# Attention block on one core: the mask instruction scales and keeps the negated maximum itself, its semaphore counts tiles, and the output banks are drained in two parts

## The chip, the core and the metric

The kernel runs on one core of a Trainium2 chip. The metric is the device time of one execution in microseconds, taken as the median of repeated runs. The engines named below are PE (TensorE, matrix products), DVE (VectorE), ACT (ScalarE), POOL (GpSimd) and SP (SyncE, which issues the DMAs). Each works through its own instructions in order, and they meet only at semaphores.

## What is computed

The reference is one transformer layer with modulation: layer norm, attention with 32 query heads that share 8 key and value heads, an output projection, a second layer norm, and a mixture of 64 expert biases chosen by the top 8 of a router. x is 4 x 512 x 512 in float32. This is the part that matters here (names shortened):

```python
q = (h @ Wq.T)            # 4 x 512 x (32 x 128), then rotary
k = rope part of (h @ Wkr.T) and (h @ Wdk.T) @ Wupk.T
v = (h @ Wdk.T) @ Wupv.T
scores = einsum('bhqd,bhkd->bhqk', q, k) / sqrt(128)
scores = where(causal, scores, -1e9)
attn = softmax(scores)
out = einsum('bhqk,bhkd->bhqd', attn, v) @ Wo.T
x = x + ga * out
# then layer norm, router softmax, top 8, x + gb * ffn
```

## The kernel before

Every float32 product is made of three products of a high and a low part (hi and lo tiles; `passes`), so each 128x512 product of PE comes three times. The work is laid out by hand as one long pipeline: 128 steps, one for each pair of batch (4) and query head (32). Step `t` belongs to unit `u = t // 4` (one key and value head of one batch) and has `h = t % 4` (the query head within the unit). The rows `MEMSET wait_slot` (L1082) are tiny instructions that carry the wait for PE's scores.

In step `t` the engines do, in this order:

- PE: the scores of tile t+1, in four pieces by query block 3, 2, 1, 0 with 512, 384, 256 and 128 keys (L460; PSUM banks s3, s2, and s1 for the last two); the query projection of tile t+3 into bank s3 (`q_proj`, L407, 12 matmuls); in steps with h = 0 a transpose of v and the key projection of the next unit (L439, L418), with h = 2 its value projection (L430); the output projection of tile t-2 into banks o0 to o3 (`out_head`, L516, summed over the unit's four heads); and the values of tile t-1 (L501, bank pv).
- DVE: `mask_and_max(t+1, 0)` (query blocks 3 and 2), the low part of the attention output of tile t-2 (OT_lo, L1118), `mask_and_max(t+1, 1)` (blocks 1 and 0), the reciprocal of the row sums (L1093), the rotary products of tile t+3 (`q_rope`, L1055 to L1057), with h = 0 also v_lo and the key's rotary products, then the 32x32 transposes of the probabilities (L1110, L1112), and with h = 1 `add_out(u-1)`: four adds that drain banks o0 to o3 into `y` (L1126).
- ACT: OT_hi (L824), PT_hi, the high part of the transposed probabilities (L820), the four exponentials of tile t+1 (L797), their normalisation (L804), qT_hi (L774), and in ten steps of each group of 16 the high part of a block of the next weights (L768).
- POOL: PT_lo in two pieces (L1451), the sum of the rotary products (L1440), qT_lo (L1445), key work, and the low part of a block of the next weights (wq_lo and others, L1436).
- SP: the transposed probabilities make a round trip through DRAM (stored at L1642, read back into PT_raw in four DMAs at L1651, after POOL has finished with PT_raw).

`mask_and_max` is where the change lies. For each query block one custom DVE instruction (L1083) reads the score bank, adds the mask, writes `probs` and keeps the row maximum, which a small read-accumulator instruction then writes to `row_max`. After two blocks the semaphore `dve_s` rises by one (two per tile), DVE waits for it itself, and a `TENSOR_SCALAR` (L1087) on two columns makes `neg_max`, which ACT waits for by `dve_nm`. PE waits for `dve_s` before it writes a bank again: for `q_proj(t+3)`, which needs s3 alone, the wait is `dve_s >= 2 * (t + 1) + 1`, and so for blocks 3 and 2 together.

From step 117 on (`FFN_FROM`) the router and expert work of one 128-row tile is woven into each step. The last three tiles are transposed by PE instead of DVE and DMA (`last_step`), and a tail of router work ends the program.

Of the kernel before, what the change touches and what calls it, by code (L numbers as in the profile page):

```python
# [12 lines left out]
P = 128  # L13
# [86 lines left out]
def build(nc, A, out):  # L100
    ctx = ExitStack()
    with ctx:
# [4 lines left out]
        class Region:  # L107
# [51 lines left out]
        rot_s = whole.take("rot_s", [P, SEQ])  # L159
        row_max, neg_max, row_sum, row_inv = (  # L160
            [whole.take(f"{n}{i}", [P, QT]) for i in range(2)] for n in ("row_max", "neg_max", "row_sum", "row_inv"))
        router_bias = whole.take("router_bias", [P, EXPERTS])
# [125 lines left out]
        def sem(name):  # L288
# [27 lines left out]
                                                  sem("act_o"))  # L316
        dve_s, dve_nm, dve_ri, dve_r, dve_o = (sem("dve_s"), sem("dve_nm"), sem("dve_ri"),
                                                      sem("dve_r"), sem("dve_o"))
# [19 lines left out]

        FFN_FROM = ALL - STEPS + GROUP + 1

        def pieces(t):
# [11 lines left out]
        def tensor_program(pe):  # L353
# [43 lines left out]
            def q_proj(t):  # L397
                b, h = t // GROUP % BATCH, t % GROUP
                if t > 0:
                    pe.wait_ge(dve_r, t)  # L400
                if t >= 3:
                    pe.wait_ge(dve_s, 2 * (t - 2) + 1)
                if b == 0:
                    pe.wait_ge(pool_w, chunk_event(t // STEPS - 1, CHUNKS.index(f"wq{h}")) + 1)
                for c in range(CH):
                    for n, (w, x) in enumerate(passes(wq, hT)):
                        mm = pe.matmul(q_bank(t)[:], w[:, h, c, :], x[:, b * CH + c, :],  # L407
                                       start=(c == 0 and n == 0), stop=(c == CH - 1 and n == 2))
                mm.then_inc(pe_qp, 1)

            def k_proj(u):
                if u > 0:
                    pe.wait_ge(dve_s, 2 * (GROUP * (u - 1) + 1) + 1)
                if u % BATCH == 0:
                    pe.wait_ge(pool_w, chunk_event(u // BATCH - 1, CHUNKS.index("wk")) + 1)
                for c in range(CH):
                    for n, (w, x) in enumerate(passes(wk, hT)):
                        mm = pe.matmul(kv_bank(u)[:], w[:, c, :], x[:, (u % BATCH) * CH + c, :],  # L418
                                       start=(c == 0 and n == 0), stop=(c == CH - 1 and n == 2))
                mm.then_inc(pe_k, 1)  # L420

            def v_proj(u):
                pe.wait_ge(dve_kr, u + 1)
                if u > 0:
                    pe.wait_ge(dve_s, 2 * (GROUP * (u - 1) + 3) + 1)
                if u % BATCH == 0:
# [7 lines left out]
            def v_transpose(u):  # L434
                pe.wait_ge(act_vraw, u + 1)
                if u > 0:
                    pe.wait_ge(dve_s, 2 * (GROUP * u + 1) + 2)
                for j in range(QT):
                    mm = pe.transpose(vt_bank(u)[:, j * P:(j + 1) * P], kv_raw[:, j * P:(j + 1) * P], ident[:])  # L439
                mm.then_inc(pe_vt, 1)  # L440

            def scores(t, tiles):
                if tiles[0] == QUERY_ORDER[0]:
# [3 lines left out]
                    if t > 0:  # L447
                        pe.wait_ge(dve_s, 2 * t)
                    if t >= 2:
# [117 lines left out]
            def step(t):  # L567
# [15 lines left out]
                if n is not None:  # L583
                    pe.wait_ge(dve_s, 2 * (t + 2))
                    if h == 0:
# [17 lines left out]
            def last_step(t):  # L603
# [20 lines left out]
                values(t)  # L624
                pe.wait_ge(dve_s, 2 * (t + 2 if has1 else t + 1))
                ffn_mix(n - 4, "s3")
# [93 lines left out]
        def scalar_program(act):  # L720
# [72 lines left out]
            def exponentials(t, half):  # L793
                m = t % 2
                act.wait_ge(dve_nm, 2 * t + half + 1)
                for qt in HALVES[half]:
                    ins = act.activation(row(t, qt), row(t, qt), ACT.Exp, bias=neg_max[m][:, qt:qt + 1], scale=SCALE,  # L797
                                         accum_out=row_sum[m][:, qt:qt + 1])
                ins.then_inc(act_exp, 1)
# [179 lines left out]
        def vector_program(dve):  # L979
# [93 lines left out]
            def mask_and_max(t, half):  # L1073
# [5 lines left out]
                for qt in HALVES[half]:  # L1079
                    if qt:  # L1080
                        dve.wait_ge(pe_s, 4 * t + (4 if qt == 1 else 4 - qt))
                        dve.memset(wait_slot[:, qt:qt + 1], 0.0)  # L1082
                    ins = dve.tensor_tensor_reduce(row(t, qt), score_bank[qt], mask[:, SEQ - (qt + 1) * P:], 1.0, LOWEST,  # L1083
                                                   ALU.add, ALU.max, row_max[m][:, qt:qt + 1])
                ins.then_inc(dve_s, 1)
                dve.wait_ge(dve_s, 2 * t + half + 1)
                dve.tensor_scalar(neg_max[m][:, half_cols(half)], row_max[m][:, half_cols(half)], -SCALE, None,  # L1087
                                  ALU.mult).then_inc(dve_nm, 1)

# [30 lines left out]

            def add_out(u):
                for j in range(QT):
                    ps = out_bank(u, j)
# [129 lines left out]
            def step(t):  # L1253
# [5 lines left out]
                if n is not None:  # L1259
                    ffn_norm(n - 1)  # L1260
                invert_sums(t + 1, 0)
                q_rope(t + 3)
# [12 lines left out]
                if h == 1 and u > 0 and not soon(t - 1):  # L1275
                    add_out(u - 1)
                if soon(t):
# [518 lines left out]
```

## Time and profile before

| | us |
|---|---|
| median of 3 runs | 1674.41 (1671.79 to 1675.16) |
| the profiled execution | 1675.79 |
| its span, first to last instruction | 1674.5 |
| PE busy (share of the span) | 1548.9 (92%) |
| DVE busy | 1272.3 (76%) |
| POOL busy | 1027.2 (61%) |
| ACT busy | 1002.1 (60%) |

A profile gives for each engine the time in which it worked, for groups of equal instructions the count, the busy time and the idle time of the engine just before them, and for a stretch of time each instruction with its start and length. Lengths of matmuls overlap, since the engine is pipelined: the distance between two starts tells what one costs.

### The profile page before, as it was taken

Reading aid. Unit: us, or ns where it says so; the run is one execution under the profiler, and the core shown is the slowest. Engines: PE = TensorE matmul, PEld = TensorE weight load, DVE = VectorE, ACT = ScalarE, POOL = GpSimd, SP = SyncE. Lnnn points to the kernel's source line nnn. Section 1 sums busy time; section 2 is a strip of 40 time slices with the busy share of each in tenths; the row PEclk is TensorE's granted clock in tenths of the full one; section 3 lists DMA queues with packets and bytes.
Section 4 is the critical chain, followed back from the end, with each engine's and each line's share of the span. In section 5 each row is a group of like instructions: output and inputs, shape, how many; then the busy total and the mean of one; then the engine's idle time right before and its main releaser. Section 6 shows DMA issues by size and latency. Waiting matters only on the chain.

```text
span 1674.5 us, 24760 instructions
## 1 busy us (share of the span) xinstructions
PE 1548.9 (92%) x7630; PEld 1294.0 (77%) x7630; DVE 1272.3 (76%) x3663; ACT 1002.1 (60%) x2333; POOL 1027.2 (61%) x774
## 2 busy tenths in 40 slices
PE   8989999999999999999999999999999999897787
PEld 5668888888888888888888888888888888676664
DVE  6867777777777777777777787777777777678698
ACT  3356667666666566666666666666665666554341
POOL 2756566655665566656666566556665566577664
PEclk9989999999999999999999999999999999999877
DMA  8434344443444344433444344434443344534311
GB/s 309 165 117 130 111 136 137 130 133 107 140 151 124 110 131 130 149 111 118 150 129 123 126 128 137 137 110 131 136 133 129 113 134 151 153 104 136 98 50 71
DMA packets 139123, 218.30 MB, mean 130 GB/s; under 512 B 29472, under 2 KB 101920, under 8 KB 138992
## 3 DMA queue, kind: packets, MB, share of 16 engines
q1 hardware_dynamic: 138672, 216.61, 41.1%
q8 instruction: 62, 1.02, 0.3%
q14 instruction: 69, 0.57, 0.1%
q10 hardware_dynamic: 320, 0.11, 0.0%
HBM read 127.38 MB, written 89.29 MB: 129 GB/s over the span
## 4 chain that ended last, share of the span: by engine, by line
PE 65%; DVE 21%; issue 10%; POOL 2%; ACT 1%; DMA 1%; DVEq 0%; SPq 0%; POOLq 0%; ACTq 0%
PE bank_s L407 22%; PE bank_o L516 14%; PE bank_pv L501 10%; PE bank_s L418 5%; PE bank_s L430 5%; PE bank_s L460 5%; DVE y L1126 4%; DVE probs L1083 3%; DVE blocks L1110 3%; DVE rot_s L1056 2%; DVE rot_c L1055 2%; DVE rot_s L1057 1%; PE bank_s L393 1%; DVE row_max L1083 1%; PE bank_s L439 1%
## 5 line engine op out<-in xcount | busy, mean ns | idle before, releaser
L1451 POOL TENSOR_TENSOR PT_lo<-PT_raw,PT_hi 128x640 fp32r<-128x640 f32 x250 | 386.2, 1567 | 122.9 <-ACT PT_hi L820 122.9
L797 ACT ACTIVATE probs<-probs,neg_max 128x512 f32<-128x512 f32 x508 | 281.3, 555 | 183.3 <-DVE neg_max L1087 173.8
L1440 POOL TENSOR_TENSOR rot_c<-rot_c,rot_s 128x512 f32<-128x512 f32 x128 | 167.1, 1305 | 275.1 <-DVE rot_s L1057 275.1
L804 ACT ACTIVATE probs<-probs,row_inv 128x512 f32<-128x512 f32 x508 | 255.2, 553 | 83.1 <-DVE row_inv L1093 83.1
L407 PE MATMUL bank_s<-hT_lo,wq_hi 128*128 128x512 f32 x500 | 207.2, 414 | 70.3 <-DVE row_max L1083 62.8
L1083 DVE CUSTOM_DVE_ANT_0 probs<-bank_s,mask 128x512 f32<-128x512 f32 x508 | 229.1, 486 | 0.1
L1445 POOL TENSOR_TENSOR qT_lo<-rot_c,qT_hi 128x512 fp32r<-128x512 f32 x128 | 166.9, 1304 | 92.8 <-ACT qT_hi L774 92.8
L1110 DVE STREAM_TRANSPOSE blocks<-probs 128x384 f32<-128x384 f32 x500 | 202.8, 443 | 6.0 <-ACT probs L804 2.9
L407 PE MATMUL bank_s<-hT_hi,wq_hi 128*128 128x512 f32 x500 | 196.4, 393 | 0.0
L516 PE MATMUL bank_o<-wo_lo,OT_hi 128*128 128x512 f32 x496 | 193.4, 390 | 3.1 <-DVE OT_lo L1118 3.1
L407 PE MATMUL bank_s<-hT_hi,wq_lo 128*128 128x512 f32 x500 | 196.2, 392 | 0.0
L516 PE MATMUL bank_o<-wo_hi,OT_hi 128*128 128x512 f32 x496 | 193.0, 389 | 0.0
L516 PE MATMUL bank_o<-wo_hi,OT_lo 128*128 128x512 f32 x496 | 193.0, 389 | 0.0
L1082 DVE MEMSET wait_slot<- 128x1 f32 x384 | 22.7, 59 | 217.8 <-PE bank_s L460 217.7
L824 ACT ACTIVATE OT_hi<-bank_pv 128x512 fp32r<-128x512 f32 x124 | 74.3, 599 | 186.3 <-PE bank_pv L501 186.3
L501 PE MATMUL bank_pv<-PT_lo,v_hi 128*128 128x512 f32 (+3 forms) x512 | 168.1, 328 | 15.2 <-POOL PT_lo L1451 6.6
L407 PEld LDWEIGHTS bank_s<-hT_lo,wq_hi 128*128 128x128 f32 x500 | 94.5, 189 | 99.6 <-issue 83.9
L820 ACT ACTIVATE PT_hi<-PT_raw 128x640 fp32r<-128x640 f32 x250 | 169.6, 729 | 0.3 <-DMA PT_raw<-blocks 0.3
L460 PE MATMUL bank_s<-kT_lo,qT_hi 128*128 128x512 f32 (+3 forms) x512 | 160.8, 314 | 8.7 <-issue 3.7
L501 PE MATMUL bank_pv<-PT_hi,v_lo 128*128 128x512 f32 (+3 forms) x512 | 168.1, 328 | 0.0
L501 PE MATMUL bank_pv<-PT_hi,v_hi 128*128 128x512 f32 (+3 forms) x512 | 167.8, 328 | 0.0
L460 PE MATMUL bank_s<-kT_hi,qT_lo 128*128 128x512 f32 (+3 forms) x512 | 166.7, 326 | 0.0
(224 smaller groups left out, 3627.6 us busy)
## 6 DMA issues: line engine op xcount, KB each, us to landing
blocks<-blocks SPq DMA_DIRECT2D x125, 640.0 KB, 2.9
PT_raw<-blocks SPq DMA_DIRECT2D x500, 160.0 KB, 3.1
stage<-in_wq SPq DMA_DIRECT2D x32, 256.0 KB, 3.5
stage<-in_wo SPq DMA_DIRECT2D x32, 256.0 KB, 3.5
wmod<-in_wmod SPq DMA_DIRECT2D x6, 1024.0 KB, 10.1
y<-in_x SPq DMA_DIRECT2D x4, 1024.0 KB, 12.2
stage<-in_x SPq DMA_DIRECT2D x16, 256.0 KB, 2.8
out_y<-h SPq DMA_DIRECT2D x16, 256.0 KB, 2.0
```

Of the source, the lines that this page charges most:

```text
L407: mm = pe.matmul(q_bank(t)[:], w[:, h, c, :], x[:, b * CH + c, :], start=(c == 0 and n == 0), stop=(c == CH - 1 and n == 2))
L460: mm = pe.matmul(score_bank[qt], q[:, qt * P:(qt + 1) * P], k[:, 0:(qt + 1) * P], start=(n == 0), stop=(n == 2))
L501: mm = pe.matmul(to, a[:, kb, :], ps, start=(kb == 0 and n == 0), stop=(kb == KEY_ORDER[-1] and n == 2))
L516: mm = pe.matmul(out_bank(u, j)[:], o[:, j * P:(j + 1) * P], w[:, h, :], start=(h == 0 and n == 0), stop=(h == GROUP - 1 and n == 2))
L797: ins = act.activation(row(t, qt), row(t, qt), ACT.Exp, bias=neg_max[m][:, qt:qt + 1], scale=SCALE, accum_out=row_sum[m][:, qt:qt + 1])
L804: ins = act.activation(row(t, qt), row(t, qt), ACT.Copy, scale=row_inv[t % 2][:, qt:qt + 1])
L820: act.activation(PT[0][:, at], PT_raw[:, at], ACT.Copy).then_inc(act_t, 1)
L1083: ins = dve.tensor_tensor_reduce(row(t, qt), score_bank[qt], mask[:, SEQ - (qt + 1) * P:], 1.0, LOWEST, ALU.add, ALU.max, row_max[m][:, qt ...
L1110: ins = dve.transpose(blocks_v[:, qt:qt + 3 * whole_keys - 2:3], keys[:, 0:whole_keys])
L1440: pool.tensor_tensor(rot_c[:], rot_c[:], rot_s[:], ALU.add).then_inc(pool_a, 1)
L1445: pool.tensor_tensor(lo[:], rot_c[:], hi[:].bitcast(F32), ALU.subtract).then_inc(pool_q, 1)
L1451: pool.tensor_tensor(PT[1][:, at], PT_raw[:, at], PT[0][:, at].bitcast(F32), ALU.subtract).then_inc(pool_t, 1)
```

## The change

The custom instruction scales by minus the softmax scale and keeps a running minimum, so that its accumulator already is the negated, scaled maximum; the two `TENSOR_SCALAR` per tile and the semaphore `dve_nm` are gone, and the exponentials take scale -1. `dve_s` now rises by one after each query block (four per tile); `score_read(t, qt)` is the count at which block `qt` of tile `t` has been read, and all waits are written by it. Each exponential has its own wait. `add_out` drains banks o0 and o1 where it stood (h = 1), and banks o2 and o3 one step later (h = 2), between the masks and the reciprocal.

```diff
+        def score_read(t, qt):
+
+            return QT * (t + 1) - qt
...
             def q_proj(t):
                 if t >= 3:
-                    pe.wait_ge(dve_s, 2 * (t - 2) + 1)
+                    pe.wait_ge(dve_s, score_read(t - 2, 3))
...
             def k_proj(u):
                 if u > 0:
-                    pe.wait_ge(dve_s, 2 * (GROUP * (u - 1) + 1) + 1)
+                    pe.wait_ge(dve_s, score_read(GROUP * (u - 1) + 1, 2))
...
             def v_transpose(u):
                 if u > 0:
-                    pe.wait_ge(dve_s, 2 * (GROUP * u + 1) + 2)
+                    pe.wait_ge(dve_s, score_read(GROUP * u + 1, 0))
...
             def exponentials(t, half):
                 m = t % 2
-                act.wait_ge(dve_nm, 2 * t + half + 1)
                 for qt in HALVES[half]:
-                    ins = act.activation(row(t, qt), row(t, qt), ACT.Exp, bias=neg_max[m][:, qt:qt + 1], scale=SCALE,
+                    act.wait_ge(dve_s, score_read(t, qt))
+                    ins = act.activation(row(t, qt), row(t, qt), ACT.Exp, bias=row_min[m][:, qt:qt + 1], scale=-1.0,
                                          accum_out=row_sum[m][:, qt:qt + 1])
                 ins.then_inc(act_exp, 1)
...
             def mask_and_max(t, half):
...
                         dve.memset(wait_slot[:, qt:qt + 1], 0.0)
-                    ins = dve.tensor_tensor_reduce(row(t, qt), score_bank[qt], mask[:, SEQ - (qt + 1) * P:], 1.0, LOWEST,
-                                                   ALU.add, ALU.max, row_max[m][:, qt:qt + 1])
-                ins.then_inc(dve_s, 1)
-                dve.wait_ge(dve_s, 2 * t + half + 1)
-                dve.tensor_scalar(neg_max[m][:, half_cols(half)], row_max[m][:, half_cols(half)], -SCALE, None,
-                                  ALU.mult).then_inc(dve_nm, 1)
+
+                    dve.tensor_tensor_reduce(row(t, qt), score_bank[qt], mask[:, SEQ - (qt + 1) * P:], -SCALE,
+                                             -LOWEST, ALU.add, ALU.min, row_min[m][:, qt:qt + 1]).then_inc(dve_s, 1)
...
-            def add_out(u):
-                for j in range(QT):
+            def add_out(u, tiles=range(QT)):
+                for j in tiles:
...
             def step(t):
                 mask_and_max(t + 1, 1)
                 if n is not None:
                     ffn_norm(n - 1)
+                if h == 2 and u > 0 and not soon(t - 2):
+                    add_out(u - 1, range(2, QT))
                 invert_sums(t + 1, 0)
...
                 if h == 1 and u > 0 and not soon(t - 1):
-                    add_out(u - 1)
+                    add_out(u - 1, range(2))
```

What this makes of the order of DVE's instructions, first where a step with h = 1 ends and the step with h = 2 begins. "ISA probs,row_max" is the mask instruction and the "ISA row_max" behind it the read of its accumulator. Before:

```order
L1126 TENSOR_TENSOR y<-bank_o,y 128x512 [waits pe_op] x4
L1082 MEMSET wait_slot 128x1 [waits pe_s,dve_tp]
L1083 ISA probs,row_max_93<-bank_s,mask 128x512
L1083 ISA row_max_93 128x1
L1082 MEMSET wait_slot 128x1 [waits pe_s]
L1083 ISA probs,row_max_93<-bank_s,mask 128x384
L1083 ISA row_max_93 128x1
L1087 TENSOR_SCALAR neg_max_95<-row_max_93 128x2 [waits dve_s]
L1118 TENSOR_TENSOR OT_lo<-bank_pv,OT_hi 128x4x4x32 [waits act_o]
L1082 MEMSET wait_slot 128x1 [waits pe_s]
L1083 ISA probs,row_max_93<-bank_s,mask 128x256
L1083 ISA row_max_93 128x1
```

And after:

```order
L1127 TENSOR_TENSOR y<-bank_o,y 128x512 [waits pe_op] x2
L1086 MEMSET wait_slot 128x1 [waits pe_s,dve_tp]
L1088 ISA probs,row_min_93<-bank_s,mask 128x512
L1088 ISA row_min_93 128x1
L1086 MEMSET wait_slot 128x1 [waits pe_s]
L1088 ISA probs,row_min_93<-bank_s,mask 128x384
L1088 ISA row_min_93 128x1
L1119 TENSOR_TENSOR OT_lo<-bank_pv,OT_hi 128x4x4x32 [waits act_o]
L1086 MEMSET wait_slot 128x1 [waits pe_s]
L1088 ISA probs,row_min_93<-bank_s,mask 128x256
L1088 ISA row_min_93 128x1
```

Two of the four adds stand ahead of the masks instead of four, and the `TENSOR_SCALAR` between block 2 and OT_lo is gone.

Further on in the step with h = 2, DVE before (the rows from block 0 to the first rotary product):

```order
L1083 ISA probs,row_max_93<-bank_s,mask 128x128
L1083 ISA row_max_93 128x1
L1087 TENSOR_SCALAR neg_max_95<-row_max_93 128x2 [waits dve_s]
L1093 RECIPROCAL row_inv_99<-row_sum_97 128x2 [waits act_exp]
L1055 TENSOR_TENSOR rot_c<-bank_s,cos_t 128x512 [waits pool_q,pe_qp]
```

And after:

```order
L1088 ISA probs,row_min_93<-bank_s,mask 128x128
L1088 ISA row_min_93 128x1
L1127 TENSOR_TENSOR y<-bank_o,y 128x512 [waits pe_op] x2
L1094 RECIPROCAL row_inv_97<-row_sum_95 128x2 [waits act_exp]
L1059 TENSOR_TENSOR rot_c<-bank_s,cos_t 128x512 [waits pool_q,pe_qp]
```

The two other adds stand between the last mask and the reciprocal, ahead of the rotary products.

ACT, the exponentials of one tile, before:

```order
L820 ACTIVATE PT_hi<-PT_raw 128x640 [waits pe_pv,d_tr0]
L820 ACTIVATE PT_hi<-PT_raw 128x640
L797 ACTIVATE probs,row_sum_96<-probs,neg_max_94 128x512 [waits dve_nm]
L797 ACTIVATE probs,row_sum_96<-probs,neg_max_94 128x384
L797 ACTIVATE probs,row_sum_96<-probs,neg_max_94 128x256 [waits dve_nm]
```

And after:

```order
L824 ACTIVATE PT_hi<-PT_raw 128x640 [waits pe_pv,d_tr0]
L824 ACTIVATE PT_hi<-PT_raw 128x640
L801 ACTIVATE probs,row_sum_94<-probs,row_min_92 128x512 [waits dve_s]
L801 ACTIVATE probs,row_sum_94<-probs,row_min_92 128x384 [waits dve_s]
L801 ACTIVATE probs,row_sum_94<-probs,row_min_92 128x256 [waits dve_s]
```

The exponential of block 2 has a wait of its own (as has that of block 0), and each waits for `dve_s`.

## Rows read from the trace of the kernel before

**Rows 1.** The page: span, chain of work that ended last, PE's longest group with its idle time.

```profile
span 1674.5 us, 24760 instructions
...
PE 65%; DVE 21%; issue 10%; POOL 2%; ACT 1%; DMA 1%; DVEq 0%; SPq 0%; POOLq 0%; ACTq 0%
...
L407 PE MATMUL bank_s<-hT_lo,wq_hi 128*128 128x512 f32 x500 | 207.2, 414 | 70.3 <-DVE row_max L1083 62.8
```

**Rows 2.** Groups by line, 400 to 1400 us: busy, mean ns, idle before and releasers.

```profile
L407 PE MATMUL bank_s<-hT_lo,wq_hi 128*128 128x512 f32 x348 | 143.2, 412 | 47.8 <-DVE row_max L1083 41.4 <-issue 3.7 <-POOL wq_lo L1436 2.7
...
L1087 DVE TENSOR_SCALAR neg_max<-row_max 128x2 f32<-128x2 f32 x174 | 95.3, 548 | 6.0
```

**Rows 3.** Timeline of all engines in a step with h = 1: start, length, instruction.

```profile
710.75 0.69 DVE L1083 CUSTOM_DVE_ANT_0 probs<-bank_s,mask 128x512 f32<-128x512 f32 x1
...
711.37 0.08 DVE L1083 DVE_READ_ACCUMULATOR2_ANT row_max<- 128x1 f32 x1
711.38 0.55 DVE L1083 CUSTOM_DVE_ANT_0 probs<-bank_s,mask 128x384 f32<-128x384 f32 x1
...
711.46 0.27 PE L460 MATMUL bank_s<-kT_hi,qT_hi 128*128 128x128 f32 x1
711.86 0.08 DVE L1083 DVE_READ_ACCUMULATOR2_ANT row_max<- 128x1 f32 x1
...
712.09 0.48 PE L407 MATMUL bank_s<-hT_lo,wq_hi 128*128 128x512 f32 x1 [0.35 <-DVE row_max L1083]
...
712.40 0.40 PE L407 MATMUL bank_s<-hT_hi,wq_lo 128*128 128x512 f32 x1
```

**Rows 4.** Timeline of all engines where the next step, h = 2, begins.

```profile
719.01 2.45 DVE L1126 TENSOR_TENSOR y<-bank_o,y 128x512 f32<-128x512 f32 x4
...
721.32 0.27 PE L460 MATMUL bank_s<-kT_hi,qT_hi 128*128 128x128 f32 x1
721.39 0.69 DVE L1083 CUSTOM_DVE_ANT_0 probs<-bank_s,mask 128x512 f32<-128x512 f32 x1
...
722.00 0.08 DVE L1083 DVE_READ_ACCUMULATOR2_ANT row_max<- 128x1 f32 x1
...
722.72 0.47 PE L407 MATMUL bank_s<-hT_lo,wq_hi 128*128 128x512 f32 x1 [1.12 <-DVE row_max L1083]
```

**Rows 5.** Timeline where step 64 (h = 0) begins, with its weight block.

```profile
835.53 1.28 POOL L1436 TENSOR_TENSOR wq_lo<-stage,wq_hi 128x512 fp32r<-128x512 f32 x1
...
836.23 0.27 PE L460 MATMUL bank_s<-kT_hi,qT_hi 128*128 128x128 f32 x1
...
836.96 0.48 PE L407 MATMUL bank_s<-hT_lo,wq_hi 128*128 128x512 f32 x1 [0.46 <-POOL wq_lo L1436]
```

**Rows 6.** Timeline of all engines around one of the small scaling instructions.

```profile
353.22 3.07 POOL L1451 TENSOR_TENSOR PT_lo<-PT_raw,PT_hi 128x640 fp32r<-128x640 f32 x2 [0.41 <-ACT PT_hi L820]
...
354.75 1.56 DVE L1087 TENSOR_SCALAR neg_max<-row_max 128x2 f32<-128x2 f32 x1
```

**Rows 7.** That instruction by its line, whole run: minimum, median, maximum ns.

```profile
L1087 DVE TENSOR_SCALAR neg_max<-row_max x256: 168/348/1616, 91.3 to 1605.0; 128x2 f32<-128x2 f32 x128
```

**Rows 8.** Another DVE instruction that reads a bank, with two operations, by tile.

```profile
L1036 DVE TENSOR_SCALAR h_raw<-bank_o,modT x8: 777/796/812, 31.3 to 96.4; 128x512 f32<-128x512 f32 x8
```

**Rows 9.** Timeline of DVE: the first rotary product of the step of rows 3.

```profile
715.14 0.69 DVE L1055 TENSOR_TENSOR rot_c<-bank_s,cos_t 128x512 f32<-128x512 f32 x1 [0.69 <-PE bank_s L407]
```

**Rows 10.** The DMAs that read PT_raw back, by line: lengths and time to landing.

```profile
L1651 SPq DMA_DIRECT2D PT_raw<-blocks x500: 302/426/1941, 104.0 to 1566.8; - x167
...
DMA to landing us min/median/max: 2.5/3.1/4.7
```

**Rows 11.** The chain of waits in the router stage at the end.

```profile
1514.21 1.05 DVE neg_max L1087
...
1546.93 1.04 DVE neg_max L1087
```

**Rows 12.** The subtraction of the router's norm on DVE, by line: minimum, median, maximum ns.

```profile
L1165 DVE TENSOR_SCALAR h<-y,small x10: 535/1549/1873, 1469.2 to 1612.8; 128x512 f32<-128x512 f32 x10
```

More of the change, by code:

```diff
@@ L159, in build @@
         rot_s = whole.take("rot_s", [P, SEQ])
-        row_max, neg_max, row_sum, row_inv = (
-            [whole.take(f"{n}{i}", [P, QT]) for i in range(2)] for n in ("row_max", "neg_max", "row_sum", "row_inv"))
+        row_min, row_sum, row_inv = (
+            [whole.take(f"{n}{i}", [P, QT]) for i in range(2)] for n in ("row_min", "row_sum", "row_inv"))
         router_bias = whole.take("router_bias", [P, EXPERTS])
@@ L316, in build @@
                                                   sem("act_o"))
-        dve_s, dve_nm, dve_ri, dve_r, dve_o = (sem("dve_s"), sem("dve_nm"), sem("dve_ri"),
+        dve_s, dve_ri, dve_r, dve_o = (sem("dve_s"), sem("dve_ri"),
                                                       sem("dve_r"), sem("dve_o"))
@@ L424, in v_proj @@
                 if u > 0:
-                    pe.wait_ge(dve_s, 2 * (GROUP * (u - 1) + 3) + 1)
+                    pe.wait_ge(dve_s, score_read(GROUP * (u - 1) + 3, 2))
                 if u % BATCH == 0:
@@ L447, in scores @@
                     if t > 0:
-                        pe.wait_ge(dve_s, 2 * t)
+                        pe.wait_ge(dve_s, score_read(t - 1, 0))
                     if t >= 2:
@@ L583, in step @@
                 if n is not None:
-                    pe.wait_ge(dve_s, 2 * (t + 2))
+                    pe.wait_ge(dve_s, score_read(t + 1, 0))
                     if h == 0:
@@ L624, in last_step @@
                 values(t)
-                pe.wait_ge(dve_s, 2 * (t + 2 if has1 else t + 1))
+                pe.wait_ge(dve_s, score_read(t + 1 if has1 else t, 0))
                 ffn_mix(n - 4, "s3")
```

## The prediction, made before the changed kernel had run

> **What bounds the kernel now.** I read the page first. The chain that ended last is PE for 65%, DVE for 21% and "issue" for 10% [rows 1], so DVE is busy for 76% of the span and yet has a hand in the end. The place where it enters is the first matmul of the query projection (L407): PE idles there for 70.3 us, nearly all of it put down to DVE's `row_max` [rows 1]. In the even stretch from 400 to 1400 us, 87 steps, it is 47.8 us [rows 2]. I then read the timeline of a short step. The last score matmul starts at 711.46, the query projection at 712.09: 0.63 us, where a 128-column matmul would let the next one start about 0.1 us later [rows 3]. What ended the wait is in the same rows: block 2's accumulator read ends at 711.94, and PE starts 0.15 us behind it. Yet PE needs only bank s3, and the read of block 3 had ended at 711.45 [rows 3].
>
> In the step that follows a step with h = 1 it is worse. DVE still drains four output banks (719.01 to 721.46), block 3's mask starts 0.07 us after the last score matmul instead of 0.71 us before it, and PE starts 1.40 us after that matmul (722.72 against 721.32) [rows 4]. The two kinds account for the stretch: 65 x 0.35 + 22 x 1.12 us of idle = 47.4 of 47.8 us [rows 2 to 4]. Elsewhere in the steady steps PE's matmuls follow each other without a hole that I could find. So PE's own work is the bound, plus this one wait in each step.
>
> **The finer semaphore.** `q_proj` now waits for block 3 alone. By the 0.15 us from the accumulator's read to PE's start, PE starts at 711.45 + 0.15 = 711.60, which is 0.14 after the last score matmul: 0.49 us earlier [rows 3]. This is on PE's own path, so it counts in full as long as nothing else is late. The other waits of PE that were rewritten (key and value projection, v transpose, next scores) stand behind 2.7 us or more of matmuls, and cost nothing before or after. The added increments I cost at nothing: they ride on instructions that are there already. From both sides: the first matmul after the wait is followed by the second 0.31 us later [rows 3], where the steady distance is 0.23; if that restart went too, up to 0.1 us a step would come on top (12 us for 120 steps); and if a mask with two working operations took longer, the nearest row is a `TENSOR_SCALAR` with two operations from a bank, 0.80 us against the mask's 0.69 for 512 columns [rows 3, 8], which costs 0.1 us a step (12 us). I take zero for both, since the mask already runs two operations (add and maximum) at 0.69 us, and PE will still stop for a moment.
>
> **The drain in two parts.** Four adds take 2.45 us, so two fewer make DVE free 1.2 us earlier at the end of a step with h = 1 [rows 4]. The mask was 0.78 us late (0.71 + 0.07), so it is on time with about 0.4 us to spare. That margin is not eaten by the faster PE: the work ahead of it hangs on the end of the query projection, and moves with it. Thus in steps with h = 2 PE starts 0.14 instead of 1.40 us after the last score matmul, 1.26 us earlier. The two moved adds now stand ahead of the reciprocal and of the rotary products in the step with h = 2. Behind them wait ACT's normalisation and `q_rope`. But DVE waits there for PE anyway: 0.69 us idle before the rotary product [rows 9], to which come the two deleted instructions. The adds (1.2 us) fit to within 0.1 us, and this step has a value projection (12 matmuls, 2.7 us) more on PE. Their cost is nothing; uncovered it would be at most 1.2 x 29 = 35 us. PE needs banks o2 and o3 only after the query and value projections, 5 us later.
>
> **The deleted instruction.** `neg_max` works on two columns, yet takes 0.168 to 1.616 us, median 0.348 [rows 7]; 95.3 us over 87 steps, 1.1 us a step [rows 2]. The rows show why: it starts at 354.75 inside POOL's subtractions and ends at 356.31, where they end (353.22 + 3.07 = 356.29) [rows 6]. The Trainium skill, "SBUF — State Buffer", section "Who interferes with whom", says that a `tensor_scalar` from SBUF to SBUF can take both port pairs, one of which GpSimd needs, so that the later of the two is blocked for a whole instruction; the trace agrees. In the steady steps this time stands behind the masks that PE waits for, and beside PE's matmuls; it frees DVE and lets the exponentials start 0.5 to 2 us earlier, but is worth nothing to the end of the step. ACT's added waits cost nothing either.
>
> In the router stage the chain does pass through it: 1.05, 0.93, 1.11, 1.04 and 0.81 us (the first and the fourth stand in [rows 11]), 4.9 us. I don't book all of it: the router's norm subtraction on DVE has a median of 1.549 and a minimum of 0.535 us [rows 12], so it waits for POOL too, and with `neg_max` gone it comes sooner into the same POOL instruction. I take half, 2.5 us, between 0 and 5. (By the skill's rule alone the wait would simply move on, and the sum would be 2.5 us less.)
>
> **Where a new wait takes over.** Seven weight groups split blocks wq1 and wq3 on POOL right before they are needed. In step 64 POOL's block ends at 836.81 and PE starts at 836.96, 0.73 us after the last score matmul [rows 5]. POOL's block too hangs on the query projection before it, so 0.73 stays. Hence 7 steps with h = 0 gain nothing, and 7 with h = 2 gain 1.40 - 0.73 = 0.67 us instead of 1.26.
>
> **The sum**, over steps 3 to 116 (114 steps; 28 with h = 2, 86 others):
> - (86 - 7) x 0.49 = 38.7 us
> - 21 x 1.26 + 7 x 0.67 = 26.5 + 4.7 = 31.2 us
> - steps 1 and 2, after the long start: about 1.2 us
> - 8 steps with router work: 8 x 0.49 = 3.9 us, and 2.5 us of `neg_max`
>
> Together 77.5 us. The profiled execution took 1675.8 us, so it becomes 1598.3; the median of the runs shown is 1.4 us below it, so 1597. Forecast 1598.
>
> **Rivals.**
> 1. The increment of block 3 isn't seen by PE before block 2 is through, since block 2's mask starts inside it (711.38 against an end of 711.44 [rows 3]) and the rows show a release only behind a read with an idle pipeline after it. Then only the late mask goes: 21 x 0.77 + 7 x 0.67 + 0.5 + 2.5 = 24 us, 1650. The skill, "VectorE: DVE Perf Modes", "The DRAIN you can't avoid", has the next instruction wait for an empty pipeline; the overlap of 0.06 us in rows 3 speaks against taking this literally. Chance 6%.
> 2. The round trip through DRAM becomes the bound. POOL's end releases four DMAs that land 3.1 us after issue, at most 4.7 [rows 10]; ACT needs them in the steps after a short one, and has about 1 us to spare now, 0.5 after. A late landing delays the exponentials, not PE; they start 0.5 us or more earlier than before, which pays for it. If half a microsecond still came through in the 58 long steps, 29 us of the gain would go: 1627. Chance 7%.
> 3. **Slower:** the mask with a scale takes longer by a whole pass, because 1.0 was a special case. With x more on the 512 columns, 79 steps gain 0.49 - x, 21 gain 1.26 - x. It decides at x of about 0.65 us: one more pass (x = 0.69) gives 79 x 0.20 - 21 x 0.57 = 4 us lost against 2.5 won, no change; two passes (x = 1.38) give 79 x 0.89 + 21 x 0.12 + 14 x 0.5 = 80 us more, about 1753. The row against it is the 0.80 us of another two-operation instruction [rows 8]. Chance 2% for no change, 3% for slower.
> 4. The change doesn't do what it says: the four increments are there in the order of the instructions, and the counts fit; I give it nothing beyond rival 1.
>
> **Chances and range.** Forecast 81%, rival 1 6%, rival 2 7%, rival 3 5% (2 + 3), 1% for causes that I don't see and that eat all. A measurement of this kernel can tell about 0.2% (3.3 us). Faster 0.94, same 0.03, slower 0.03. The forecast's own bounds are 1598 - 12 (restart) - 2.5 and 1598 + 12 (mask) + some 5 for a margin of 0.4 us that isn't always there; with part of rival 2 the range is 1582 to 1622.
>
> **What would show it.** L407's idle before falls from 70.3 to about 12 us; PE starts 0.14 us behind the last score matmul in short and long steps alike, 0.73 in the 14 with a weight block; the 512-column mask stays at 0.69 us; the drain shows as two groups of two; exponentials start right after PT_hi; in the router stage the norm subtraction grows. Wrong would be: a start still 0.15 us behind block 2's read (rival 1), ACT waiting for PT_raw and PE for DVE behind it (rival 2), longer masks (rival 3).

## The result and the profile after

The changed kernel takes 1596.7 us (median of 4 runs, 1595.67 to 1598.29) against 1673.58 us of the kernel before beside it; the ratio is 0.9542, 95% interval 0.9525 to 0.9558. The forecast was 1598 us, with a range of 1582 to 1622.

The page of the changed kernel, the lines that answer to [rows 1] (its lines have moved: the query projection is now L411, the scores L464, the mask L1088, the drain L1127). What `dve_s` counts are query blocks, four per tile, and not tiles as the title has it:

```profile
span 1594.4 us, 24504 instructions
PE 1527.3 (96%) x7630; PEld 1286.5 (81%) x7630; DVE 1135.2 (71%) x3407; ACT 983.0 (62%) x2333; POOL 1027.7 (64%) x774
...
PE 80%; DVE 7%; POOL 7%; issue 3%; ACT 2%; DMA 1%; SPq 0%; DVEq 0%; POOLq 0%; ACTq 0%
...
L411 PE MATMUL bank_s<-hT_lo,wq_hi 128*128 128x512 f32 x500 | 206.0, 412 | 10.8 <-POOL wq_lo L1439 6.4
```

The idle time of PE ahead of the query projection is 10.8 us where it was 70.3, and 6.4 us of what is left are put down to POOL's weight block. DVE's share of the chain has fallen from 21% to 7%. DVE has 137 us less work (1135.2 against 1272.3).

A step with h = 1 in the timeline of all engines (start, length, instruction), step 53, the same as in [rows 3]:

```profile
678.22 0.69 DVE L1088 CUSTOM_DVE_ANT_0 probs<-bank_s,mask 128x512 f32<-128x512 f32 x1
...
678.83 0.08 DVE L1088 DVE_READ_ACCUMULATOR2_ANT row_min<- 128x1 f32 x1
678.84 0.55 DVE L1088 CUSTOM_DVE_ANT_0 probs<-bank_s,mask 128x384 f32<-128x384 f32 x1
...
678.93 0.27 PE L464 MATMUL bank_s<-kT_hi,qT_hi 128*128 128x128 f32 x1
679.06 0.47 PE L411 MATMUL bank_s<-hT_lo,wq_hi 128*128 128x512 f32 x1
679.13 0.71 ACT L801 ACTIVATE probs<-probs,row_min 128x512 f32<-128x512 f32 x1
679.32 0.09 DVE L1088 DVE_READ_ACCUMULATOR2_ANT row_min<- 128x1 f32 x1
...
679.38 0.39 PE L411 MATMUL bank_s<-hT_hi,wq_lo 128*128 128x512 f32 x1
```

PE starts at 679.06, 0.15 us behind the end of block 3's accumulator read (678.83 + 0.08) and 0.26 us before that of block 2 begins (679.32); it is 0.13 us behind the last score matmul (0.63 before). The first exponential starts right there too, at 679.13, 0.20 us behind the last score matmul; before, it started 1.37 us behind it. The second matmul of the projection still comes 0.32 us after the first.

Where the next step, h = 2, begins, as in [rows 4]:

```profile
685.93 1.25 DVE L1127 TENSOR_TENSOR y<-bank_o,y 128x512 f32<-128x512 f32 x2
...
687.50 0.06 DVE L1086 MEMSET wait_slot<- 128x1 f32 x1 [0.31 <-PE bank_s L464]
687.54 0.69 DVE L1088 CUSTOM_DVE_ANT_0 probs<-bank_s,mask 128x512 f32<-128x512 f32 x1
...
688.15 0.08 DVE L1088 DVE_READ_ACCUMULATOR2_ANT row_min<- 128x1 f32 x1
...
688.25 0.27 PE L464 MATMUL bank_s<-kT_hi,qT_hi 128*128 128x128 f32 x1
688.38 0.47 PE L411 MATMUL bank_s<-hT_lo,wq_hi 128*128 128x512 f32 x1
```

Two adds, then DVE is idle for 0.31 us before the wait instruction, and the mask starts 0.71 us ahead of the last score matmul: PE starts 0.13 us behind it (1.40 before). Step 64 keeps its wait for the weight block, as in [rows 5]:

```profile
796.17 1.30 POOL L1439 TENSOR_TENSOR wq_lo<-stage,wq_hi 128x512 fp32r<-128x512 f32 x1
...
796.88 0.27 PE L464 MATMUL bank_s<-kT_hi,qT_hi 128*128 128x128 f32 x1
...
797.61 0.47 PE L411 MATMUL bank_s<-hT_lo,wq_hi 128*128 128x512 f32 x1 [0.46 <-POOL wq_lo L1439]
```

797.61 - 796.88 is 0.73 us, as before.

### The profile page after: what moved, and what is told of

Read it like the earlier page. It is cut to its first block, busy times and chain, and to the rows that moved or that the text cites. A ratio compares the mean times of both kernels' runs of the same rounds, so it can differ in the third digit from the quotient of the medians.

```text
span 1594.4 us, 24504 instructions
## 1 busy us (share of the span) xinstructions
PE 1527.3 (96%) x7630; PEld 1286.5 (81%) x7630; DVE 1135.2 (71%) x3407; ACT 983.0 (62%) x2333; POOL 1027.7 (64%) x774
## 4 chain that ended last, share of the span: by engine, by line
PE 80%; DVE 7%; POOL 7%; issue 3%; ACT 2%; DMA 1%; SPq 0%; DVEq 0%; POOLq 0%; ACTq 0%
PE bank_s L411 22%; PE bank_o L520 18%; PE bank_pv L505 13%; PE bank_s L464 12%; PE bank_s L422 5%; PE bank_s L434 5%; POOL rot_c L1443 1%; POOL qT_lo L1448 1%; POOL wq_lo L1439 1%; PE bank_s L397 1%; POOL PT_lo L1454 1%; PE bank_s L443 1%; DVE rot_s L1060 1%; DVE rot_s L1061 1%; ACT qT_hi L778 1%
## 5 line engine op out<-in xcount | busy, mean ns | idle before, releaser
L801 ACT ACTIVATE probs<-probs,row_min 128x512 f32<-128x512 f32 x508 | 278.5, 552 | 18.8 <-DVE row_min L1088 18.4
L1088 DVE CUSTOM_DVE_ANT_0 probs<-bank_s,mask 128x512 f32<-128x512 f32 x508 | 229.5, 488 | 1.5 <-issue 1.2
L411 PE MATMUL bank_s<-hT_lo,wq_hi 128*128 128x512 f32 x500 | 206.0, 412 | 10.8 <-POOL wq_lo L1439 6.4
L411 PE MATMUL bank_s<-hT_hi,wq_lo 128*128 128x512 f32 x500 | 195.4, 391 | 0.0
L411 PE MATMUL bank_s<-hT_hi,wq_hi 128*128 128x512 f32 x500 | 195.3, 391 | 0.0
L1059 DVE TENSOR_TENSOR rot_c<-bank_s,cos_t 128x512 f32<-128x512 f32 x125 | 86.4, 691 | 138.9 <-PE bank_s L411 138.9
L464 PE MATMUL bank_s<-kT_lo,qT_hi 128*128 128x512 f32 (+3 forms) x512 | 160.7, 314 | 9.9 <-issue 3.7
L464 PE MATMUL bank_s<-kT_hi,qT_lo 128*128 128x512 f32 (+3 forms) x512 | 166.6, 325 | 0.0
```

The source lines that it names most:

```text
L464: mm = pe.matmul(score_bank[qt], q[:, qt * P:(qt + 1) * P], k[:, 0:(qt + 1) * P], start=(n == 0), stop=(n == 2))
L801: ins = act.activation(row(t, qt), row(t, qt), ACT.Exp, bias=row_min[m][:, qt:qt + 1], scale=-1.0, accum_out=row_sum[m][:, qt:qt + 1])
```

## The experiments

Each kernel has one part of the change alone, or the changed kernel with one part undone or altered. Read from the timelines of all of them, this is the distance from the last score matmul to the query projection (median of the steps of a kind), and the length of three stretches: steady steps (from step 2 to step 116), steps with router work (116 to 124), and the rest behind step 124's scores. All in us.

| kernel | h = 0, 1, 3 | h = 2 | before wq1, wq3 | steady | router steps | rest | median time |
|---|---|---|---|---|---|---|---|
| before | 0.63 | 1.40 | 1.36, 0.73 | 1311.0 | 125.6 | 114.4 | 1672 to 1675 |
| scale only (e3) | 0.63 | 1.40 | 1.36, 0.73 | 1310.4 | 124.6 | 110.1 | 1668.4 |
| drain only (e2) | 0.63 | 0.63 | 0.74, 0.73 | 1290.1 | 125.5 | 112.8 | 1651.4 |
| count only (e1) | 0.14 | 0.91 | 0.87, 0.73 | 1258.7 | 124.4 | 115.3 | 1620.6 |
| whole drain (e4) | 0.14 | 0.91 | 0.87, 0.74 | 1257.4 | 125.6 | 107.4 | 1613.6 |
| scaling kept (e5) | 0.14 | 0.14 | 0.73, 0.74 | 1241.1 | 124.0 | 115.2 | 1603.1 |
| changed kernel | 0.14 | 0.14 | 0.73, 0.73 | 1240.6 | 123.8 | 107.8 | 1596.7 |
| drain 3 + 1 (e6) | 0.14 | 0.32 | 0.74, 0.73 | 1244.8 | 122.9 | 109.1 | 1600.7 |
| blocks early (e7) | 0.14 | 0.14 | 0.11, 0.11 | 1231.4 | 123.8 | 109.1 | 1587.6 |
| scaling for tiles 125 to 127 (e8) | 0.14 | 0.14 | 0.74, 0.73 | 1241.0 | 125.6 | 111.9 | 1600.9 |
| scaling for tiles 0 to 124 (e9) | 0.14 | 0.14 | 0.75, 0.73 | 1241.4 | 124.5 | 109.8 | 1599.8 |

**The count by blocks alone.** The kernel before with this edit (and the waits of PE by `score_read`); the scaling instruction waits for the block that ends its half:

```diff
-                ins.then_inc(dve_s, 1)
-                dve.wait_ge(dve_s, 2 * t + half + 1)
+                    # inside the loop over the blocks of the half: .then_inc(dve_s, 1)
+                dve.wait_ge(dve_s, score_read(t, HALVES[half][1]))
```

> Kernel before with one part alone: dve_s counts query blocks (four per tile) and PE's waits go by it; the small scaling instruction and its semaphore stay, the drain stays whole at h = 1. My theory: PE starts 0.49 us earlier in steps of every kind, since the late mask in steps with h = 2 stays late (0.07 + 0.69 + 0.15 = 0.91 us behind the last score matmul instead of 1.40); 7 steps with h = 0 gain nothing because of the weight block. (114 - 7) x 0.49 = 52 us, about 1 us at the start, 0 to 4 in the router stage: 1673.6 - 55 = 1619. Rival (an increment is only seen behind the next mask): 1673. Rival (the count needs the deleted instruction too, to keep DVE on time): less than 30 us of gain.

Measured 1620.64 us, ratio 0.9693 (0.9678 to 0.9707). Its timeline of all engines where step 54 (h = 2) begins:

```profile
695.73 0.27 PE L464 MATMUL bank_s<-kT_hi,qT_hi 128*128 128x128 f32 x1
695.80 0.68 DVE L1088 CUSTOM_DVE_ANT_0 probs<-bank_s,mask 128x512 f32<-128x512 f32 x1
...
696.41 0.08 DVE L1088 DVE_READ_ACCUMULATOR2_ANT row_max<- 128x1 f32 x1
...
696.64 0.47 PE L411 MATMUL bank_s<-hT_lo,wq_hi 128*128 128x512 f32 x1 [0.64 <-DVE row_max L1088]
```

The mask is as late as before (0.07 us behind the last score matmul), PE follows block 3's read by 0.15 us, at 0.91. The increment is seen while block 2's mask runs, and the count doesn't need the other two parts. It is 52 of the 70 us that the steady steps gave back.

**The drain in two parts alone.**

```diff
+                if h == 2 and u > 0 and not soon(t - 2):
+                    add_out(u - 1, range(2, QT))
                 invert_sums(t + 1, 0)
...
-                    add_out(u - 1)
+                    add_out(u - 1, range(2))
```

> Kernel before with one part alone: the drain of the output banks in two parts (o0, o1 at h = 1; o2, o3 at h = 2). My theory: the mask of block 3 is on time at h = 2, so that PE starts 0.63 instead of 1.40 us behind the last score matmul: 21 x 0.77 + 7 x 0.67 = 21 us, 1652. Rival (the two adds push the rotary products at h = 2, where the scaling instructions still take time, and something behind them comes late): 1660 to 1674.

Measured 1651.36 us, ratio 0.9871 (0.9854 to 0.9889). PE starts 0.63 us behind the last score matmul in steps with h = 2, too. The moved adds cost nothing even where the scaling instructions still stand before them; the steady stretch is 20.9 us shorter, 21 were worked out.

**The scaled mask alone.**

```diff
-                    ins = dve.tensor_tensor_reduce(row(t, qt), score_bank[qt], mask[:, SEQ - (qt + 1) * P:], 1.0, LOWEST,
-                                                   ALU.add, ALU.max, row_max[m][:, qt:qt + 1])
+                    ins = dve.tensor_tensor_reduce(row(t, qt), score_bank[qt], mask[:, SEQ - (qt + 1) * P:], -SCALE,
+                                                   -LOWEST, ALU.add, ALU.min, row_min[m][:, qt:qt + 1])
                 ins.then_inc(dve_s, 1)
-                dve.wait_ge(dve_s, 2 * t + half + 1)
-                dve.tensor_scalar(neg_max[m][:, half_cols(half)], row_max[m][:, half_cols(half)], -SCALE, None,
-                                  ALU.mult).then_inc(dve_nm, 1)
```

> Kernel before with one part alone: the mask instruction scales and keeps the minimum, the scaling instruction is gone; the semaphore still counts halves and the drain is whole. My theory: nothing in the steady steps (PE waits for block 2's read, which doesn't move), 0 to 5 us in the router stage: 1669 to 1674, most likely 1671. Rival (the deleted instruction was the main part of the gain, because the 1.1 us that DVE spent on it in each step were on the path): 1640 or less.

Measured 1668.4 us, ratio 0.9975 (0.9964 to 0.9985). The page of this kernel:

```profile
PE 1544.6 (93%) x7630; PEld 1291.2 (77%) x7630; DVE 1135.0 (68%) x3407; ACT 992.6 (59%) x2333; POOL 1027.0 (62%) x774
...
L411 PE MATMUL bank_s<-hT_lo,wq_hi 128*128 128x512 f32 x500 | 207.1, 414 | 70.6 <-DVE row_min L1088 63.0
```

DVE works 137 us less, and PE is still idle for 70.6 us there, 63.0 of them put down to DVE: the work taken away didn't stand on the path, and the steady steps moved by 0.6 us in 1311. The rest of its gain lies behind step 116 (5.3 us in the profiled executions).

**The changed kernel with the scaling instruction kept**, that is count and drain together (the mask with 1.0 and the maximum, and the `TENSOR_SCALAR` behind each half).

> Changed kernel with one part undone: the mask keeps the maximum and the small scaling instruction is back, with the count by blocks and the drain in two parts. My theory: the steady steps stay as in the changed kernel (0.14 us behind the last score matmul), because OT_lo, the later masks and the adds have room on DVE; only the router stage loses 0 to 5 us: 1597 to 1602. Rival (with the adds ahead of the rotary products, DVE at h = 2 is late without the deletion): 1605 or more, and PE waiting for DVE in the trace.

Measured 1603.12 us, 6.4 us more than the changed kernel (ratio to before 0.9587, 0.9573 to 0.9602), a little over the 0 to 5 expected. The steady steps are 0.5 us longer; nearly all lies behind step 124, in the rest.

**The changed kernel with the whole drain at h = 1.**

```diff
-                if h == 2 and u > 0 and not soon(t - 2):
-                    add_out(u - 1, range(2, QT))
...
-                    add_out(u - 1, range(2))
+                    add_out(u - 1)
```

> Changed kernel with one part undone: all four adds of the drain at h = 1 again. My theory: the mask of block 3 is 0.78 us late at h = 2, since the adds hang on the rotary products and those on PE: PE starts 0.91 instead of 0.14 us behind the last score matmul in 21 steps, and 0.91 instead of 0.73 in 7: 21 x 0.77 + 7 x 0.18 = 17.4 us more, 1614. Rival (the scaling instruction's absence already frees DVE enough for four adds): 1597.

Measured 1613.57 us, ratio 0.9636 (0.9623 to 0.9649). In its timeline of all engines, where step 54 begins, the adds end 0.15 us behind the start of the last score matmul (692.39 + 2.45 against 694.69), and the mask starts 0.07 us behind it instead of 0.71 us ahead, although no scaling instruction stands on DVE any more:

```profile
692.39 2.45 DVE L1127 TENSOR_TENSOR y<-bank_o,y 128x512 f32<-128x512 f32 x4
...
694.69 0.27 PE L464 MATMUL bank_s<-kT_hi,qT_hi 128*128 128x128 f32 x1
694.76 0.68 DVE L1088 CUSTOM_DVE_ANT_0 probs<-bank_s,mask 128x512 f32<-128x512 f32 x1
...
695.38 0.08 DVE L1088 DVE_READ_ACCUMULATOR2_ANT row_min<- 128x1 f32 x1
...
695.60 0.47 PE L411 MATMUL bank_s<-hT_lo,wq_hi 128*128 128x512 f32 x1 [0.64 <-DVE row_min L1088]
```

**Three adds at h = 1 and one at h = 2.**

```diff
-                    add_out(u - 1, range(2, QT))
+                    add_out(u - 1, range(3, QT))
...
-                    add_out(u - 1, range(2))
+                    add_out(u - 1, range(3))
```

> Changed kernel with three adds at h = 1 and one at h = 2. It measures the margin on DVE, which I estimated at 0.4 us with two adds (an add takes 0.6). My theory: the mask is late by 0.6 - 0.4 = 0.2 us in 28 steps; in the 7 with a weight block the wait for POOL hides it: 21 x 0.2 = 4 us more, 1601. Rival (margin of 0.6 us or more): 1597.

Measured 1600.71 us, ratio 0.9562 (0.9549 to 0.9575), 4.0 us more. Timeline of all engines, step 54:

```profile
689.62 0.69 DVE L1088 CUSTOM_DVE_ANT_0 probs<-bank_s,mask 128x512 f32<-128x512 f32 x1
...
690.14 0.27 PE L464 MATMUL bank_s<-kT_hi,qT_hi 128*128 128x128 f32 x1
...
690.46 0.47 PE L411 MATMUL bank_s<-hT_lo,wq_hi 128*128 128x512 f32 x1
```

The mask starts 0.52 us ahead of the last score matmul instead of 0.71, so it is 0.19 us late, and PE's start moves from 0.13 to 0.32 by the same amount. The margin with two adds was 0.4 us, as worked out from an add of 0.6.

**Weight blocks one step earlier.** This takes away what makes PE wait for POOL in 14 steps:

```diff
-CHUNK_STEP = {0: [0], 1: [1], 2: [2], 3: [3], 10: [4], 11: [5], 12: [6], 13: [7], 14: [8], 15: [9]}
+CHUNK_STEP = {0: [0], 1: [1], 2: [2], 3: [3], 9: [4], 10: [5], 11: [6], 12: [7], 13: [8], 14: [9]}
```

> Changed kernel with the splitting of the six weight blocks of the next group one step earlier (steps 9 to 14 of 16 instead of 10 to 15). It takes away the wait for POOL that I found in 14 steps (0.73 us behind the last score matmul instead of 0.14): 14 x 0.59 = 8.3 us less, 1588.5. Rival (POOL's block in other short steps delays PT_lo or the rotary sum, and PE waits for that): 1597 or more.

Measured 1587.57 us, ratio 0.9478 (0.9463 to 0.9492): 9 us below the changed kernel (8.3 were worked out), and the fastest of all. Its timeline, where step 64 begins, and its page:

```profile
788.99 1.30 POOL L1448 TENSOR_TENSOR qT_lo<-rot_c,qT_hi 128x512 fp32r<-128x512 f32 x1 [0.74 <-ACT qT_hi L778]
...
790.70 1.58 POOL L1454 TENSOR_TENSOR PT_lo<-PT_raw,PT_hi 128x640 fp32r<-128x640 f32 x1 [0.42 <-ACT PT_hi L824]
...
790.95 0.27 PE L464 MATMUL bank_s<-kT_hi,qT_hi 128*128 128x128 f32 x1
791.06 0.45 PE L411 MATMUL bank_s<-hT_lo,wq_hi 128*128 128x512 f32 x1
```

```profile
PE 1524.0 (96%) x7630; PEld 1285.6 (81%) x7630; DVE 1134.7 (72%) x3407; ACT 982.6 (62%) x2333; POOL 1028.3 (65%) x774
...
PE 86%; DVE 5%; POOL 4%; issue 3%; ACT 1%; DMA 1%; SPq 0%; DVEq 0%; POOLq 0%; ACTq 0%
...
L411 PE MATMUL bank_s<-hT_lo,wq_hi 128*128 128x512 f32 x500 | 205.1, 410 | 3.3 <-DVE row_min L1088 3.3
```

No weight block lies between qT_lo and PT_lo, and PE's idle time before the projection is down to 3.3 us.

**Where the scaling instruction costs.** Two kernels ask where its 6.4 us lie: the changed kernel with the instruction back for tiles 125 to 127 alone (6 of them), and for tiles 0 to 124 alone (250 of them).

```diff
+                if t >= 125:    # the other kernel: t < 125
+                    dve.wait_ge(dve_s, score_read(t, HALVES[half][1]))
+                    dve.tensor_scalar(row_min[m][:, half_cols(half)], row_max[m][:, half_cols(half)], -SCALE, None,
+                                      ALU.mult).then_inc(dve_nm, 1)
```

> Changed kernel with the small scaling instruction back for tiles 125 to 127 alone (6 instructions; in the kernel before they took 3.4 us together). It asks where the 6.4 us lie that keeping the instruction everywhere cost. My theory: in the last three tiles, where PE transposes the probabilities itself and the softmax is on the path, so nearly all of it comes back: 1596.7 + 3.4 to 6.4 = 1600 to 1603, and the stage behind the last query projection grows from about 108 us to 112 to 115. Rival (it lies in the router steps 117 to 124, as I predicted): within 1.5 us of 1597.

> Changed kernel with the small scaling instruction back for tiles 0 to 124 (250 instructions, some 135 us of DVE's time), and not for the last three. My theory: no effect on the steady steps and at most 1 us in the router steps, where the waits are POOL's: 1597 to 1598. Rival (the router steps hold the cost): 1600 to 1603.

Measured 1600.87 us (ratio 0.9562, 0.9549 to 0.9576) and 1599.84 us (0.9559, 0.9546 to 0.9572). Six instructions cost 4.2 us, 250 cost 3.1, and the two together make 7.3 against the 6.4 of all 256. These are differences of medians; by the ratios to the kernel before beside each they are 3.3 and 2.8 us, and 7.5 for all 256, with intervals of about 2 us on each ratio. So it is clear that the instruction costs several microseconds, and not how they are split to the microsecond. The theory of the last tiles held in its time (1600 to 1603 expected; the rest took 111.9 us where 112 to 115 were expected), and the expected 0 to 1 us for the others didn't: of the two expectations for that kernel, the rival's 1600 to 1603 is the nearer, though not by its reason. The 3.1 us have no single place in the profiled execution: 0.8 us in the steady steps, 0.7 in the router steps, 2.0 in the rest, where this kernel has no such instruction and only what is late from before can tell. Of those 2.0 us 0.6 can be found: in step 124 the mask of block 3 starts 0.11 us ahead of the last score matmul (1488.05 against 1488.16) instead of 0.71 ahead (1485.86 against 1486.57), and the last query projection waits 0.45 us for it, 0.73 us behind that matmul instead of 0.14. What carries the others stays open; the differences between single profiled executions of kernels without the instruction are as large (122.9 to 125.6 for the router steps, 107.4 to 110.1 for the rest).

## Why the prediction came out right

**The bound and the semaphore.** The reading of [rows 3] holds to a hundredth: PE follows the accumulator read of the block that it waits for by 0.15 us, in the changed kernel behind block 3, and starts 0.14 us behind the last score matmul (the median of the steps that have no other wait). The count alone gave 52.3 us of the steady stretch; 52 was expected for it.

**The drain.** The term was 0.78 us of lateness at h = 2 with 0.4 us to spare afterwards. The whole drain put back costs 16.9 us (17.4 worked out), and the third add costs 0.19 us a step (0.2 worked out). That the margin doesn't shrink when PE gets faster is shown by the count alone: the mask at h = 2 stays 0.07 us behind the last score matmul, although every step is 0.49 us shorter. The work ahead of it hangs on the query projection and moves with it.

**The weight blocks.** 0.73 us stayed in 14 steps, and went when the blocks moved.

**The steady sum.** Steps 2 to 116 went from 1311.0 to 1240.6 us, 70.4 less; the sum had 69.9 for steps 3 to 116. What lies ahead gave 1.2 us, as in the sum: step 2's last score matmul stood at 123.4 and stands at 122.2.

**The bounds.** The restart of PE stayed (0.32 us between the first two matmuls, 0.31 before), so nothing of the 12 us below came. The mask instruction with scale and minimum is as long as before: by shape its mean was 690, 553, 419 and 283 ns for 512, 384, 256 and 128 columns, and is 692, 554, 420 and 287. Its line in the changed kernel (minimum, median, maximum ns):

```profile
L1088 DVE CUSTOM_DVE_ANT_0 probs<-bank_s,mask x508: 279/486/692, 90.2 to 1526.8; 128x512 f32<-128x512 f32 x43, 128x128 f32<-128x128 f32 x43, 128x256 f32<-128x256 f32 x42, 128x384 f32<-128x384 f32 x42
```

So nothing of the 12 us above, and none of rival 3, came either. Rival 1 (increment seen late) is excluded by the 0.15 us. Rival 2 (round trip through DRAM) didn't decide: ACT waited for PT_raw 1.0 us in the whole run, 0.3 before, in this line of the page:

```profile
L824 ACT ACTIVATE PT_hi<-PT_raw 128x640 fp32r<-128x640 f32 x250 | 169.7, 730 | 1.0 <-DMA PT_raw<-blocks 1.0
```

**Two terms at the end were mis-sized**, and their errors cancel in part: 6.4 us were booked for them, and the last two stages of the profiled executions got 8.4 us shorter. In all, the profiled execution went down by 80.1 us where the sum had 77.5. That the median came within 1.3 us of the forecast is therefore partly luck: the profiled execution before was 2.2 us above the median of its kernel and the one after 1.0 us below, and the working itself ended at 1597, not at the 1598 given as the forecast. The windows of the last two stages, before and after (length, busy time of PE, PE's weight loads, DVE, ACT and POOL with counts, granted clock, DMA share and rate):

```profile
1434.40:1560.10 125.70, 105.29 (x518) 86.27 (x516) 100.68 (x282) 63.16 (x155) 88.35 (x74) 0.96 0.45 129
1560.10:1674.50 114.40, 90.74 (x379) 63.61 (x377) 90.26 (x248) 34.35 (x100) 64.33 (x62) 0.80 0.22 71
```

```profile
1362.80:1486.60 123.80, 104.26 (x517) 86.09 (x515) 91.70 (x266) 62.55 (x155) 88.32 (x74) 0.96 0.47 133
1486.60:1594.40 107.80, 86.23 (x379) 59.84 (x377) 85.47 (x239) 34.24 (x100) 65.11 (x62) 0.83 0.22 73
```

For the eight steps with router work the sum had 3.9 us from the count; they gave 1.8 (125.6 by the starts, 123.8). The step that failed is "8 x 0.49". PE does start earlier: the distances from the last score matmul to the query projection add up to 3.5 us less over these steps, yet the stage is only 1.8 us shorter. The other kernels say the same: at a granted clock of 0.95 or 0.96 the stage takes 122.9 to 124.5 us in six kernels with the count by blocks, 123.9 in the mean, and 124.6, 125.5 and 125.6 in the three without; the two kernels with the count that take 125.6 (e4, e8) have a clock of 0.93 there. That POOL is what absorbs the gain is an inference, not shown by an experiment: POOL is busy for 88.3 of 123.8 us, and the chain of waits of the changed kernel runs through it for a part of these steps:

```profile
1446.02 1.26 POOL h L1490
...
1447.35 1.28 POOL h L1492
1448.63 1.24 POOL rot_c L1443
```

For `neg_max` the sum had 2.5 us and the runs show 6.4. I had looked at the instruction's own length in the chain and halved it. Four of the five places that I had added up lie ahead of 1560.10, in the router steps, so the term was also put into the wrong stage: most of the cost shows in the rest behind step 124. There PE transposes the probabilities itself and the softmax of one tile stands between two products; with the instruction kept the chain runs from it through ACT's exponentials and normalisation, here in the kernel that keeps it:

```profile
1533.98 0.80 DVE neg_max L1091
...
1534.81 0.98 ACT probs L801 x4
1535.80 0.84 ACT probs L808 x2
...
1536.82 0.79 ACT probs L808 x2
```

Across all kernels the rest takes 107.4 to 110.1 us where the last three tiles have no scaling instruction, and 111.9 to 115.3 where they have it. The instructions themselves last 3.4 us together in the kernel before. Part of the rest goes with the granted clock, as the windows of this stage show for the kernel with all of the instructions kept, and then for the one with those of tiles 125 to 127:

```profile
1488.10:1603.30 115.20, 90.29 (x380) 63.79 (x378) 90.28 (x248) 34.36 (x100) 64.33 (x62) 0.79 0.21 70
...
1488.80:1600.70 111.90, 86.87 (x380) 60.83 (x378) 89.55 (x247) 34.47 (x100) 65.13 (x62) 0.83 0.23 70
```

The latter has the clock of the changed kernel (0.83) and takes 111.9 us, 4.1 more than 107.8, and 2.1 to 2.8 more than the three other kernels at 0.83 that have no such instruction there (109.1, 109.1 and 109.8). At 0.81 the drain alone, with the instruction, takes 112.8 us, and the scaled mask alone, without it, 110.1. So at the same clock the instruction is worth 2 to 4 us in the rest. The former takes 3.3 us more again, at a clock of 0.79 (a mean over stretches at the two levels, 1.2 and 2.4 GHz), and PE needs 90.3 instead of 86.9 us for the same 380 matmuls. Whether the instruction has a part in that lower clock, or only chance, these runs don't settle. The prediction had also worked out what would follow from the lock on the shared ports alone (the Trainium skill, "SBUF — State Buffer", section "Who interferes with whom"): that the wait would simply move on to another instruction, and the term be nothing. That conclusion didn't hold here, though nothing here speaks against the lock itself. The sign that the prediction named for it, a longer norm subtraction of the router, didn't come either: its median (L1166) is 1.215 us against 1.549 in [rows 12]:

```profile
L1166 DVE TENSOR_SCALAR h<-y,small x10: 541/1215/1957, 1396.4 to 1534.1; 128x512 f32<-128x512 f32 x10
```

## What to carry to other kernels

When the bound engine waits for another at the same place in each step, look at which instruction really makes its operand free, and at what stands between that and the semaphore: here 0.49 us a step lay in one more block counted under the same number. Work that is taken from an engine beside the path is worth nothing by its amount (137 us of DVE time for 4 to 6 us), while two adds of 1.2 us together, moved into the next step once every four steps, gave 17 to 21. Where the margin ahead of such a wait hangs on the bound engine's own progress, as here, it didn't shrink when that engine got faster.

## What the runs showed of the hardware that I had not expected

That a change of some microseconds in the last stage comes with another granted clock there: 0.80 before and 0.83 after for the same 379 matmuls, whose busy time fell from 90.74 to 86.23 us. Over all eleven kernels the clock of this stage lies between 0.78 (count only, 115.3 us) and 0.85 (whole drain, 107.4 us). And that six instructions on 128x2 values, some 3 us long together, cost about 4 us of the whole where they stand between a score product and its exponential. Such an instruction lasts from 0.168 us up to 1.671 us; the long ones end with the POOL instruction, or the piece of it, that runs beside them (its line in the kernel that keeps it):

```profile
L1091 DVE TENSOR_SCALAR neg_max<-row_max x256: 168/349/1671, 91.7 to 1534.0; 128x2 f32<-128x2 f32 x128
```
